# A selective scan in a two-layer network: u broadcast in fp32 by 32-row selections, delta stored twice, new places for the preparation steps

## The reference

```python
delta = jax.nn.softplus(jnp.einsum('blr,dr->bld', dt, dt_w) + dt_b)
A = -jnp.exp(A_log)
dA = jnp.exp(delta[..., None] * A)
dBu = delta[..., None] * Bm[:, :, None, :] * xi[..., None]

def step(h, inp):
    dA_t, dBu_t, C_t = inp
    h = dA_t * h + dBu_t
    return (h, jnp.einsum('bds,bs->bd', h, C_t))
```

## Time and profile before

| | us |
|---|---|
| median of 3 runs | 5675.06 |
| lowest and highest | 5672.62, 5676.45 |
| the profiled execution, its own time | 5685.29 |
| its span | 5683.5 |
| DVE busy (share of the span) | 3950.0 (69%) |
| PE busy | 3607.9 (63%) |
| ACT busy | 2759.5 (49%) |
| POOL busy | 2643.2 (47%) |

### The profile page before, as it was taken

The page is one execution under the profiler, slowest core; times in us unless marked ns, Lnnn a source line. Parts: engine busy times, 40 slices in busy tenths (PEclk is TensorE's granted clock), DMA queues, the critical chain, the costliest instruction groups (busy, mean ns, idle before and its releaser), DMA issues.

```text
span 5683.5 us, 44812 instructions
## 1 busy us (share of the span) xinstructions
PE 3607.9 (63%) x11400; PEld 1333.7 (23%) x11400; DVE 3950.0 (69%) x3478; ACT 2759.5 (49%) x3178; POOL 2643.2 (47%) x1276
## 2 busy tenths in 40 slices
PE   6566675666756667566675666656667566675666
PEld 2211222112321123211232112321123211232112
DVE  6478675786757867578675776748766487665876
ACT  4454454444544445444454544554545545455444
POOL 2266432664336643366433664336643365433664
PEclk8677786777767778677776777767777777776777
DMA  1367303663036630466304663046630466304762
GB/s 30 85 162 175 90 12 91 163 167 90 12 97 162 162 91 11 104 157 163 90 10 109 157 164 86 8 109 161 159 87 7 109 168 159 83 4 111 172 160 68
DMA packets 186995, 597.66 MB, mean 105 GB/s; under 512 B 30956, under 2 KB 31704, under 8 KB 185912
## 3 DMA queue, kind: packets, MB, share of 16 engines
q1 hardware_dynamic: 186680, 594.18, 42.5%
HBM read 485.03 MB, written 46.14 MB: 93 GB/s over the span
## 4 chain that ended last, share of the span: by engine, by line
issue 31%; PE 23%; DVE 21%; POOL 11%; ACT 9%; DMA 4%; SPq 1%; DVEq 0%; POOLq 0%; ACTq 0%
DVE ps L1152 7%; POOL arena L1242 5%; DVE arena L1157 4%; PE ps L620 4%; PE ps L612 4%; DVE arena L1045 3%; DMA arena<-dl 3%; POOL arena L1225 3%; PE ps L516 3%; POOL arena L1231 2%; PE ps L464 2%; PE ps L562 2%; PE ps L507 2%; PE ps L640 1%; ACT arena L746 1%
## 5 line engine op out<-in xcount | busy, mean ns | idle before, releaser
L1242 POOL TENSOR_TENSOR arena<-arena 128x1024 f32<-128x1024 f32 x768 | 1799.8, 2350 | 1268.1 <-DVE arena L1157 872.7
L1157 DVE TENSOR_TENSOR_SCAN arena<-arena,ps 128x1024 f32<-128x1024 f32 x768 | 1756.3, 2287 | 151.2 <-POOL arena L1242 38.1
L640 PE MATMUL ps<-arena,spread 96*128 96x512 bf16 x1536 | 611.5, 499 | 1115.5 <-DVE arena L1157 964.2
L880 ACT ACTIVATE arena<-arena,a_all 128x1024 f32<-128x1024 f32 x768 | 872.8, 1143 | 782.1 <-DMA arena<-dl 624.8
L1152 DVE TENSOR_TENSOR ps<-ps,arena 128x1024 f32<-128x1024 f32 x768 | 929.9, 1211 | 420.9 <-PE ps L640 420.9
L658 PE MATMUL ps<-arena,gather 128*32 128x512 f32 x3072 | 725.6, 846 | 83.1 <-POOL arena L1242 83.1
L1186 POOL TENSOR_TENSOR x<-x,arena 96x512 f32<-96x512 f32 x128 | 209.4, 1636 | 848.7 <-DVE arena L963 848.7
L640 PEld LDWEIGHTS ps<-arena,spread 96*128 96x128 bf16 x1536 | 120.7, 109 | 1778.4 <-DVE arena L1157 1328.1
L612 PE MATMUL ps<-arena,w_in 96*96 96x512 f32 x512 | 367.3, 885 | 63.2 <-DMA arena<-xq 63.2
L620 PE MATMUL ps<-arena,w_in 96*96 96x512 f32 x256 | 223.6, 1022 | 252.6 <-ACT arena L843 252.6
L1134 DVE TENSOR_TENSOR arena<-ps,arena 96x1024 f32<-96x1024 f32 x64 | 78.1, 1220 | 370.2 <-ACT arena L864 370.2
(11 more groups left out here) (149 smaller groups left out, 5409.6 us busy)
## 6 DMA issues: line engine op xcount, KB each, us to landing
arena<-dl SPq DMA_DIRECT2D x768, 512.0 KB, 5.4
arena<-bc SPq DMA_DIRECT2D x128, 512.0 KB, 6.2
arena<-arena SPq DMA_DIRECT2D x576, 64.0 KB, 2.2
dl<-arena SPq DMA_DIRECT2D x64, 384.0 KB, 3.5
xq<-in_x SPq DMA_DIRECT2D x8, 1536.0 KB, 8.9
arena<-xq SPq DMA_DIRECT2D x64, 192.0 KB, 3.8
out<-x SPq DMA_DIRECT2D x64, 192.0 KB, 2.1
arena<-xq SPq DMA_DIRECT2D x64, 191.8 KB, 3.2
```

The source lines that it names most:

```text
L640: mm = pe.matmul(ps[:, bank + c, :], spread[:, r, :], sp[:, i, b, c * 512:(c + 1) * 512], start=True, stop=True)
L880: act.activation(da[:, m % DAS, :], dbc[:, m % DBC, :], ACT.Exp, scale=a_all[:, v // 2, m:m + 1]).then_inc(da_ready, 1)
L1157: dve.tensor_tensor_scan(hs[:, m % 2, :], da[:, m % DAS, :], driven, 0.0, ALU.mult, ALU.add).then_inc(h_ready, 1)
L1242: pool.tensor_tensor(pr[:, m % PRS, :], hs[:, m % 2, :], cmat[:, v % 2, :], ALU.mult).then_inc(pr_ready, 1)
```

## The change

- **u.** The split is gone: no bf16 parts, no `sp`, no `L869`, `L872`, `L1228`, `L1231`. u stays fp32 in a double buffer `u`, and one DMA per unit copies the second half (columns 512 to 1023) of its 96 rows to partitions 32 to 127 of `u_low`. `broadcast_u` is now two fp32 matmuls with 32 contraction rows each: the first half reads rows 32b to 32b+31 of `u`, the second reads rows 32(b+1) to 32(b+1)+31 of `u_low`. So the two stand in neighbouring groups of 32 rows of the array.
- **Rows.** Within the 128 rows of a step the channel is now the slow index and the state the fast one (`state_row`, `a_log`). B and C are therefore read as 16 rows repeated 8 times. Delta is stored twice, in two copies side by side, and each of the 16 stored rows is broadcast to 8 partitions. B and C are issued apart.
- **Buffers.** `dbc` has four buffers instead of three.
- **Slots.** Every engine has its own slot numbers. z moves from slot 1 to slot 2 on PE, delta from slot 4 to slot 5 on DVE, the gate from after step 2 to after step 1. On ACT the silu of xi waits for an old `y_acc`, and only the silu of z waits for `yz_ready`.

```diff
-DBC = 3
+DBC = 4
+COPIES = 2
-S_XI, S_SILU, S_DT, S_SOFT, S_U, S_R, S_P2 = 0, 1, 3, 4, 5, 6, 7
-S_GATE, S_SKIP, S_OUT = 2, 4, 8
+PE_XI, PE_Z, PE_DT = 0, 2, 3
+ACT_SILU, ACT_DT, ACT_SOFT = 1, 3, 4
+DVE_DELTA = 5
+POOL_U = 5
+SP_SHIFT, SP_BC, SP_DL, SP_B, SP_C = 5, 6, 7, 8, 10
+SP_U = 10
+S_GATE, S_SKIP, S_OUT = 1, 4, 8
...
-                    for c in range(2):
-                        mm = pe.matmul(ps[:, bank + c, :], spread[:, r, :],
-                                       sp[:, i, b, c * 512:(c + 1) * 512], start=True, stop=True)
+                    rows = [slice((b + c) * BLK, (b + c + 1) * BLK) for c in range(2)]
+                    pe.matmul(ps[:, bank, :], spread[rows[0], r, :], u[rows[0], i, 0:512], start=True, stop=True)
+                    mm = pe.matmul(ps[:, bank + 1, :], spread[rows[1], r, :], u_low[rows[1], i, :],
+                                   start=True, stop=True)
...
-                                   a["dl"][v % 2][g * DG:(g + 1) * DG, :].rearrange("(o d) n -> o d n", o=1)
-                                   .broadcast_to([NS, DG, L])).then_inc(dbc_in[m % DBC], 16)
+                                   a["dl"][v % 2][g * DG:(g + 1) * DG].rearrange("d c (o n) -> (d c) o n", o=1)
+                                   .broadcast_to([DG * COPIES, NS // COPIES, L])).then_inc(dbc_in[m % DBC], 16)
...
+                        sync.dma_start(bmat[:, i, :], a["bc"][i][0:NS, :].rearrange("(o s) n -> o s n", o=1)
+                                       .broadcast_to([DG, NS, L])).then_inc(b_in, 16)
...
+                    if slot == SP_U:
+                        sync.wait_ge(u_ready, V + 1)
+                        sync.dma_start(u_low[BLK:128, i, :], u[:, i, 512:1024]).then_inc(u_low_in[i], 16)
...
-                    if slot == S_SILU:
+                    if slot == ACT_SILU:
                         act.preload_act_table(ACT.Silu)
                         if v >= 2:
-                            act.wait_ge(yz_ready, V - 1)
+                            act.wait_ge(y_acc, (V - 2) * GPB + 1)
```

More of the change, by code:

```diff
@@ L46 @@
 BLK = 32
-NB = DI // BLK
+ROWG = 128 // BLK
 GPB = BLK // DG
@@ L184, in program @@
         soft = cut(DI, L)
-        u = soft
-        parts = [cut(DI, L // 2, BF16) for _ in range(3)]
+        u = two_of(cut(DI, 2 * L))
+        u_low = cut(128, 2 * 512).rearrange("p (i n) -> p i n", i=2)
         dbc = cut(128, DBC * L).rearrange("p (b n) -> p b n", b=DBC)
@@ L391, in prep @@
                     q, i = divmod(v, 2)
-                    if slot == S_DT + 1:
+                    if slot == SP_SHIFT and v + 1 < UNITS and v >= 1:
+                        shifted(v + 1)
+                    if slot == SP_BC:
                         sync.wait_ge(bc_evac, V + 1)
                         sync.dma_start(a["bc"][i], bc_rows).then_inc(bc_out, 16)
[L395 to L399, removed]
+                    if slot == SP_B:
                         sync.wait_ge(bc_out, (V + 1) * 16)
@@ L402, in prep @@
                         if v >= 2:
-                            sync.wait_ge(pr_ready, (V - 1) * G)
[L404 to L413, removed]
+                            sync.wait_ge(bu_ready, (V - 1) * G)
+                        sync.dma_start(bmat[:, i, :], a["bc"][i][0:NS, :].rearrange("(o s) n -> o s n", o=1)
+                                       .broadcast_to([DG, NS, L])).then_inc(b_in, 16)
+                    if slot == SP_DL:
+                        sync.wait_ge(delta_ready, V + 1)
+                        for c in range(COPIES):
+                            sync.dma_start(a["dl"][i][:, c, :], delta).then_inc(delta_out, 16)
+                    if slot == SP_C:
+                        if v >= 2:
+                            sync.wait_ge(pr_ready, (V - 1) * G)
+                        sync.dma_start(cmat[:, i, :], a["bc"][i][NS:2 * NS, :].rearrange("(o s) n -> o s n", o=1)
+                                       .broadcast_to([DG, NS, L])).then_inc(c_in, 16)
+                    if slot == SP_U:
+                        sync.wait_ge(u_ready, V + 1)
+                        sync.dma_start(u_low[BLK:128, i, :], u[:, i, 512:1024]).then_inc(u_low_in[i], 16)
                 def first():
@@ L1222, in prep @@
                     i = v % 2
[L1223 removed]
+                    if slot == POOL_U:
                         pool.wait_ge(delta_ready, V + 1)
[L1225 to L1231 removed]
+                        if v >= 2:
+                            pool.wait_ge(ubc_ready, (V - 1) * G)
+                        pool.tensor_tensor(u[:, i, :], delta, xi[:, i, :], ALU.mult).then_inc(u_ready, 1)
                 def step(v, m):
@@ L1261, in constants @@
     two_of = lambda t: np.kron(np.eye(2, dtype=np.float32), t)
-    state_row = np.arange(128) % DG
-    spread = np.zeros((R, GPB, 128), np.float32)
+    state_row = np.arange(128) // NS
+    spread = np.zeros((128, GPB, 128), np.float32)
     for r in range(GPB):
-        for k in range(3):
+        for k in range(ROWG):
             spread[k * BLK + DG * r + state_row, r, np.arange(128)] = 1.0
```

62 lines of the change are left out of this document (20 added, 42 removed).

## The result

The changed kernel takes **6091.84 us** (median of 4 runs, 6080.94 to 6101.39), against 5674.52 for the kernel before on the same chip. The ratio is 1.0735, 95% interval 1.0713 to 1.0757: it is slower, where I had forecast 5360 and called slower one case in twenty. The kernel before was timed again beside each group of experiments, with medians from 5674.5 to 5681.2, so a difference of a few us between two experiments says nothing.

A forecast was written before the change was run, and what follows sets the result against it. No engine was full; DVE's 493 us of waits inside units, largely a four-engine loop, were the bound. 493 - 151 (gate) - 39 (u's DMA) + 8 (stage start) = 311 off 5685.3: 5374, given as 5360; 8-in-10 range 5245 to 5490.

The forecast's parts named there:

- delta, inside units: DVE's wait before the delta addition: dt's chain ends at T+24.0, needed at T+25.2, so taken as 0.
- scan, for POOL: DVE's scan waiting for POOL's product: the 38 us go because the split of u goes.
- DMA: SP's queue: u's transfer lands late for the next unit's first broadcast, 0.7 us x 56 = 39 us.
- rival 3: B and C transfers use only half of the DMA engines: 2.1 us x 56 = +118, 5480 us; chance 16%.
- The broadcast behind delta: PE's broadcast for the product after delta: the prediction gave it no wait of its own.
- Gate: DVE's gate after step 1 waits for the last states on PE: 2.8 us a unit, 151 us together.
- Rival 2: PE's clock rises and xi may run at full clock, so the gate waits less: 5215 us; chance 10%.
- Start of a stage: Start of the eight scan stages: the split goes but stores stand ahead, -1 us a pair, -8 us.
- The loop: Gate, silu of xi, z and broadcast delay the fourth product by 5.46 us a unit; the new order removes this.
- The halves: PE's two fp32 broadcast matmuls run beside each other in different array rows, 0.94 us a broadcast.
- rival 1: The two broadcast halves run in series on PE, +0.94 us a broadcast: 180 us, 5540 us; chance 10%.
- The fp32 broadcast: PE's broadcast in fp32 instead of bf16: +0.4 us each (+0.9 at half clock), counted in the gate's wait.

The follow-up runs named there:

- e9: e1 with B and C each fetched by two transfers of 8 rows instead of one of 16 rows; 5899.8 us.
- e1: Changed kernel with the old row order and old transfers of B, C and delta (delta stored once), all else as changed; 5506.8 us.
- e4: Kernel before with only the new slots (z, delta, gate, the silu's wait), keeping bf16 broadcast, old rows and DMAs; 5378.4 us.
- e5: e1 with both halves of a broadcast read from the same 32 rows of u, so they cannot overlap; 5846.9 us.
- e10: e1 with the gate moved back behind step 2; 5394.9 us.
- e8: e4 with the gate moved back behind step 2, as in the kernel before; 5273.2 us.
- e12: e1 with delta stored twice and read as 16 rows each broadcast to 8 partitions; prices transfers only, rows do not fit; 5568.0 us.

## Why the prediction was wrong, by its own steps

The span's growth can be set against the waits that I had forecast for DVE:

| DVE's wait | forecast, us | measured, us |
|---|---|---|
| first product, for u | 0.7 x 56 = 39 | 446 |
| the other products, for the broadcast | 0 | 752.2 - 446 - 158 = 148 |
| gate | 151 | 248.5 |
| delta, inside units | 0 | 258.2 - 8 x 28.6 = 29 |
| scan, for POOL | 0 | 11.6 |
| start of eight stages | 8 x (13.33 + 28.67) - 8 = 328 | 158 + 8 x 28.6 = 387 |

The 446 and the 158 are the waits of the first products, added up from DVE's timeline. The differences make 752 us. Of these, 49 were there before, at the ends of the stages, and stood in no count of mine. The other 703 us are what the forecast missed: 6080.9 - 5374 = 707 between the two profiled executions (732 between the median and the 5360 that I gave).

- **DMA: the step that failed.** I had its mechanism, as the upper end of a term and as the third rival, but took 0.7 us between 0 and 2.8 "since the queue is idle between some of these issues". It isn't: six issues in 6 us, full engines, and u last. The first delta transfer was late too: it went out at T+34.7 (1154.48 - 1119.74, from the unit's first product) instead of T+32.6. The size failed too. I gave B and C 2.1 us more each by their own duration, and carried over a full rate for all the others (15.4 GB/s an engine). Measured, the full queue moved 171 GB/s, u landed 17.5 us after its issue, and the wait added 8.4 us to the median unit, 446 us in all. e9 puts the half engines, with the two issues more that it has, at 393 us, where rival 3 said 118 + 39. Without the new transfers the forecast would still have missed: e1 takes 5507.
- **The broadcast behind delta: a term left out.** I followed broadcasts 2 to 4 and stopped. Broadcast 6 stands behind skip and states, 3.73 + 3.37 us with PE at the lower level of its clock. 123 us of the table's 148 are waits of this product. In e4, with the same slots and the bf16 broadcast, it waits 8 us, so the slots alone do not make it.
- **Gate: right mechanism, size 2.8, measured 3.7.** xi took 5.5 to 7.1 us in the 49 units that have all eight records, never the 5.29 that I had put into the mean: in the unit shown PE stands for 8.27 us before it, and the granted clock of the stretch behind (1120 to 1128 us) is 0.50, the lower of its two levels. Rival 2, the clock, fell for this reason. 98 us over the forecast, of which 49 are the 8 x 6.2 us at the end of a stage (v = 7) that were there already before.
- **Start of a stage: wrong sign.** I had -1 us a pair; u's wait there went from 13.33 to 158/8 = 19.7, and again the broadcast waits for u's DMA; e9 has 16.4 there and e1 11.9.
- **The loop: right.** The wait of the fourth product is gone, and e4 alone gives 296 us, of which the gate's wait is already paid.
- **The halves: right**, the broadcast costs about 1 us (e5). The price of rival 1 was too small, 180 where e5 gives 340: a broadcast of 1.9 us stands in the way in 334 of the 768 steps and not before the gate alone.
- **The fp32 broadcast, taken at no loss but the gate's**: it costs 122 us against bf16 with the same slots (e10, e8), u's transfer included.

The range ended at 5490. It took the half engines' case with its own small price, and so what I had called possible lay outside it.

## What to carry to other kernels

When the outermost dimension of a transfer changes from 16 to 8, count it as a change of the queue for everything issued behind it, above all for the last and smallest transfer. In this queue, full for a stretch, the half-rate transfers cost what was waited for at its end (393 us in e9), not their own added duration (the forecast's 118). Moving the awaited transfer forward, one constant, gave 474 of the 585 us that undoing all the new transfers gave. And a new position for a closing step, as the gate, has to be read against the last producer in PE's queue, unit by unit to the end of its steps.

## What the runs showed of the hardware

- Transfers whose outermost dimension is 8 come with a plateau near one half in the DMA share, where the other transfers seem to have ended: 0.50 and 0.51 in the changed kernel at 128 to 155 GB/s, 0.52 in e9 at 122. With them among others the share is full, but 16 busy engines moved 171 GB/s (changed kernel) and 200 (e9), where e1's moved 236 and e12's 243.
- Two fp32 matmuls of 32 rows and 512 columns in neighbouring row groups start 0.01 us apart and take about 1.05 us for both at full clock (1128.24 to 1129.30), where two in the same rows take 1.9 (1079.80 to 1081.71 in e5).
- xi, the same eight records in every unit, ran at either level of PE's granted clock. In the changed kernel, behind PE's wait for u, it took 5.5 us or more in all 49 complete groups. In the kernel before it took 3.60 us, all of it at full clock, in 6 of 52. In e5 it took 3.68 in 22 of 50; in the one shown, PE had worked without a pause since 331.59.

```profile
331.59 2.07 PE L641 MATMUL ps<-arena,spread 32*128 32x512 f32 x2 [3.17 <-DVE arena L1152]
333.45 1.91 PE L642 MATMUL ps<-arena,spread 32*128 32x512 f32 x2
335.29 3.64 PE L660 MATMUL ps<-arena,gather 128*32 128x512 f32 x12
338.86 1.37 PE L641 MATMUL ps<-arena,spread 32*128 32x512 f32 x4
339.94 1.15 PE L642 MATMUL ps<-arena,spread 32*128 32x512 f32 x4
341.02 3.68 PE L612 MATMUL ps<-arena,w_in 96*96 96x512 f32 x8
```
